# Macaron block with routed experts: router transposes two units later, dense outputs spread, first scatter in three steps, second roots on VectorE

## The reference, cut to what matters

```
x = x + 0.5 * ffn(layernorm(x))
x = x +       attention(layernorm(x))
x = x + 0.5 * ffn(layernorm(x))

ffn:  logits = x @ router_w.T ; e = argmax(logits)          # one of 8 experts per row
      out = square(relu(x @ fc[e])) @ proj[e]               # 128 -> 512 -> 128
attention: q, k = split(x @ Wqk + bqk); v = k; 16 heads of 8 channels
      causal windows of max(4, 128 / 2**h) keys for head h
      out = softmax(q k' / sqrt(8), masked) v
      gates = softmax(x @ Wgate + bgate)  (one per head)
      result = (out * gates) @ Wproj + bproj
```

## Time and profile before

| | |
|---|---|
| median of three runs | 444.68 us (442.11 to 444.8) |
| profiled execution | 440.26 us, of which the span is 438.5 us |
| mean granted TensorE clock in it | 0.952 |
| PE busy | 357.5 us, 82% of the span |
| DVE busy | 281.5 us, 64% |
| ACT busy | 263.5 us, 60% |
| POOL busy | 256.1 us, 58% |

### The profile page before, as it was taken

One profiled execution on the slowest core, in us unless ns is written; L12 is line 12 of the kernel. 1 busy time (PEld: TensorE's weight loads), 2 busy tenths in 40 slices (PEclk: granted clock), 3 DMA queues, 4 the chain that ended last, 5 costly groups with the idle time before them and its releaser, 6 DMA issues.

```text
span 438.5 us, 9118 instructions
## 1 busy us (share of the span) xinstructions
PE 357.5 (82%) x2634; PEld 333.2 (76%) x2643; DVE 281.5 (64%) x617; ACT 263.5 (60%) x684; POOL 256.1 (58%) x289
## 2 busy tenths in 40 slices
PE   5951049999998798779999999999475699999990
PEld 5941049999998477568879797989474699999990
DVE  4696014545566486999777979899996555545540
ACT  3370077667676586445787878686363367677650
POOL 5227747000174778487483847574977977765451
PEclk9999999999999999996999999999696599999996
DMA  9993113222242287417081822224022545722210
GB/s 244 405 270 91 54 54 102 77 66 61 78 120 73 67 184 153 100 33 161 19 169 29 172 61 40 58 41 98 12 100 96 140 125 160 198 82 63 58 29 1
DMA packets 82492, 45.40 MB, mean 104 GB/s; under 512 B 47117, under 2 KB 77455, under 8 KB 82209
## 3 DMA queue, kind: packets, MB, share of 16 engines
q1 hardware_dynamic: 77312, 34.38, 31.3%
q0 software_dynamic: 4864, 10.51, 7.6%
q10 hardware_dynamic: 288, 0.19, 0.2%
HBM read 24.48 MB, written 21.01 MB: 104 GB/s over the span
## 4 chain that ended last, share of the span: by engine, by line
PE 53%; POOL 20%; issue 9%; DVE 6%; ACT 5%; DMA 4%; SPq 1%; POOLq 0%; ACTq 0%; DVEq 0%
PE bank L1355 14%; PE bank L1346 14%; POOL rows_d L527 7%; PE bank L1433 5%; POOL late_rows_d L527 4%; POOL late L546 4%; PE bank L1465 3%; PE bank L1317 3%; PE bank L1443 2%; PE bank L1337 2%; PE bank L1306 2%; ACT sq L643 2%; ACT rows L626 2%; POOL rstd L574 2%; DMA rows<-in_x 1%
## 5 line engine op out<-in xcount | busy, mean ns | idle before, releaser
L1013 DVE TENSOR_SCALAR hT<-bank 128x512 f32<-128x512 f32 x80 | 55.3, 691 | 69.2 <-PE bank L1346 69.0
L1346 PE MATMUL bank<-xT,fcb 128*128 128x128 f32 x640 | 88.3, 283 | 5.6 <-ACT xT L659 5.6
L1355 PE MATMUL bank<-wo,hT 128*128 x640 | 87.9, 281 | 2.3 <-ACT hT L675 2.3
L1346 PEld LDWEIGHTS bank<-xT,fcb 128*128 128x128 f32 x640 | 81.2, 199 | 6.4 <-ACT xT L659 6.4
L1355 PEld LDWEIGHTS bank<-wo,hT 128*128 128x128 f32 x640 | 78.5, 193 | 3.1 <-issue 3.1
L669 ACT ACTIVATE fcb<-fc 128x512 f32 x80 | 50.2, 629 | 45.9 <-PE bank L1346 45.5
L546 POOL DMA_INDIRECT late<-y_d,slot x32 | 31.1, 973 | 51.1 <-DMA y_d<-ys 41.8
L537 POOL DMA_INDIRECT out_rows<-late x40 | 39.3, 983 | 24.9 <-DVE late L1022 17.9
L675 ACT ACTIVATE hT<-hT 128x512 f32<-128x512 f32 x80 | 50.1, 627 | 5.6 <-DVE hT L1013 5.2
L1433 PE MATMUL bank<-kT,qT 128*128 128x128 f32 (+4 forms) x256 | 48.5, 318 | 2.3 <-ACT late L754 2.0
L754 ACT ACTIVATE late<-bank,nmax 128x128 f32<-128x128 f32 (+2 forms) x128 | 46.5, 408 | 5.7 <-DVE nmax L1075 4.3
(11 more groups left out here) (158 smaller groups left out, 712.2 us busy)
## 6 DMA issues: line engine op xcount, KB each, us to landing
ks<-k_d SPq DMA_DIRECT2D x32, 192.0 KB, 3.3
late_rows_d<-hT SPq DMA_DIRECT2D x5, 1028.0 KB, 7.7
rows_d<-late SPq DMA_DIRECT2D x2, 1280.0 KB
xs<-rows_d SPq DMA_DIRECT2D x20, 128.0 KB
y_d<-ys SPq DMA_DIRECT2D x40, 64.0 KB
xs<-late_rows_d SPq DMA_DIRECT2D x20, 128.0 KB
fc<-in_w_fc SPq DMA_DIRECT2D x1, 2048.0 KB, 15.7
k_d<-qkg SPq DMA_DIRECT2D x8, 192.0 KB, 2.2
```

Of the source, the lines that this page charges most:

```text
L1013: nc.vector.tensor_scalar(hT[:, v, :, :].rearrange("p k c -> p (k c)"), bank[v][:, :], 0.0, None, ALU.max).then_inc(r_s, 1)
L1346: mm = pe.matmul(bank[v][:, k * 128:(k + 1) * 128], fcb[:, v, k * 128:(k + 1) * 128], xT[:, v, :], start=True, stop=True)
L1355: mm = pe.matmul(bank[OUT_BANK[f] + v][:, 0:128], hT[:, v, k, :], wo[:, ds(e, 1), k, :], start=(k == 0), stop=(k == KT - 1))
```

## The change

Four parts.

- The first segment's scatter is issued in three steps of six tiles, each with its own wait for the normalising, which now signals after each six tiles; the semaphore's later counts are raised to match.
- The second segment's roots are computed by DVE with `spread`, behind `place_blocks(0, 1)`, instead of by POOL. POOL has one root less there. ACT does the second segment's normalising behind the mask casts instead of ahead of them.
- The router's transposes, copies and logits are placed at slots 3, 4 and 4, 5 instead of 1, 2 and 2, 3, except in batch 6.
- `outputs(i, 0)` and `outputs(i, 1)`, which stood one behind the other in slot 3 ahead of `turn_probs`, are placed in slot 2 and in slot 3, behind `turn_probs` and the projections.

```diff
 # POOL
-            for h in range(2):
-                roots(h + 1, SEG[0][h])
-                if h == 0:
-                    pool.wait_ge(zero_s, 48)
-                scatter(0, h, SEG[0][h], h + 1)
+            roots(1, SEG[0][0])
+            pool.wait_ge(zero_s, 48)
+            for k in range(3):
+                scatter(0, 0, slice(6 * k, 6 * k + 6), k + 1)
+            scatter(0, 1, SEG[0][1], 4)
             gather(0, 0, 14)
-            roots(3, LN2[0])
+            roots(2, LN2[0])
...
 # ACT
-            def normalise_rows(h, t0, t1):
-
-                act.wait_ge(root_s, h + 1)
+            def normalise_rows(r, t0, t1):
+
+                act.wait_ge(*r)
                 for t in range(t0, t1):
                     ins = act.activation(xn[:, t, :], xn[:, t, :], ACT.Copy, scale=rstd[:, t:t + 1])
-                if t1 == SEG[0][h].stop:
-                    ins.then_inc(norm_s, 1)
+                ins.then_inc(norm_s, 1)
...
-                if i >= 2 and n in (1, 2):
-                    route_copy(1, 2 * (i - 2) + n - 1, (2, 2))
+                at = 1 if i == 6 else 3
+                if i >= 2 and n in (at, at + 1):
+                    route_copy(1, 2 * (i - 2) + n - at, (2, 2))
...
                 if g >= 13:
-                    normalise_rows(0, 6 * (g - 13), 6 * (g - 12))
+                    normalise_rows((root_s, 1), 6 * (g - 13), 6 * (g - 12))
...
-            normalise_rows(1, SEG[0][1].start, N_TILES)
-
             act.wait_ge(late_const_s, 16)
             act.activation(identb[:, :], ident, ACT.Copy).then_inc(masks_s, 1)
             a, b_ = CONST_AT["mask_first"][0], CONST_AT["mask_rest"][1]
             act.activation(maskb[:, :], cst[:, a:b_], ACT.Copy).then_inc(masks_s, 1)
+            normalise_rows((rstd_s, 1), SEG[0][1].start, N_TILES)
...
 # DVE
-            scaled_variance(3, SEG[0][1])
             choose(0, 1, 3)
             count_blocks(0, 1, 3)
             bases(0, 1)
             place_tokens(0, 1, 3)
             place_blocks(0, 1)
+            spread(3, SEG[0][1])
...
 # PE, slot (i, n)
                 if n == 0 and i:
                     outputs(i - 1, 3)
-                if n == 3:
-                    outputs(i, 0)
-                    outputs(i, 1)
                 if n == 5:
                     outputs(i, 2)
                 turn_probs(i, n)
...
+                if n in (2, 3):
+                    outputs(i, n - 2)
                 if i >= 2:
-                    g = 2 * (i - 2)
-                    if n in (2, 3):
-                        route_logits(1, g + n - 2, 2)
-                    if n in (1, 2):
-                        route_turn(1, g + n - 1, (2, 2))
+                    g, at = 2 * (i - 2), 1 if i == 6 else 3
+                    if n in (at + 1, at + 2):
+                        route_logits(1, g + n - at - 1, 2)
+                    if n in (at, at + 1):
+                        route_turn(1, g + n - at, (2, 2))
```

More of the change, by code:

```diff
@@ L342, in normalise_batch @@
         def normalise_batch(eng, i):
-            eng.wait_ge(root_s, len(SEG[0]) + 1 + [4 * i < tiles.stop for tiles in LN2].index(True))
+            eng.wait_ge(root_s, len(SEG[0]) + [4 * i < tiles.stop for tiles in LN2].index(True))
             if i:
@@ L579, in window @@
                 if i in (0, 2):
-                    roots(4 + i // 2, LN2[1 + i // 2])
+                    roots(3 + i // 2, LN2[1 + i // 2])
                 if i + 2 < B:
@@ L586, in window @@
                 if 3 <= i:
-                    roots(3 + i, batch(i - 3))
-                    normalise(pool, 1, (root_s, 3 + i), batch(i - 3))
+                    roots(2 + i, batch(i - 3))
+                    normalise(pool, 1, (root_s, 2 + i), batch(i - 3))
                 add_output_bias(i)
@@ L606, in _ @@
             pool.wait_ge(no_token_s, 16 * -(-NB // FILL))
-            scatter(1, 0, slice(0, 16), 6)
-            scatter(1, 0, batch(4), 7)
+            scatter(1, 0, slice(0, 16), 8)
+            scatter(1, 0, batch(4), 9)
             for i in range(5, B):
-                roots(i + 6, batch(i))
-                normalise(pool, 1, (root_s, i + 6), batch(i))
-            scatter(1, 1, SEG[1][1], 10)
+                roots(i + 5, batch(i))
+                normalise(pool, 1, (root_s, i + 5), batch(i))
+            scatter(1, 1, SEG[1][1], 12)
             put_out(range(NB))
```

## The result

The changed kernel took 449.06 us (median of 5 runs, 445.58 to 450.16) and the kernel before 444.68 (5 runs, 442.11 to 446.08): a ratio of 1.0088, 95% interval 1.0045 to 1.0131. The forecast was 440.5. Medians are of all runs, while a ratio leaves out the executions in a slower state that every kernel shows now and then. The profiled execution took 445.58 for a span of 443.8; 5.3 more than the 438.5 of before. Both profiles are of the fastest run of their kernel: the profile of before has a mean granted TensorE clock of 0.952, while 28 runs of it on the last chip have 0.921 to 0.944.

A forecast was written before the change was run, and what follows sets the result against it. PE was taken to bound the attention loop, with POOL ending stretches at the start. Start -7.7 plus attention +3.6 gave -4.1 us: 440.5 from the median 444.68, range 435 to 446.

The forecast's parts named there:

- -4.1: Whole kernel: -7.7 us for the start plus 3.6 for the attention loop, so a faster kernel.
- The start: First feed-forward stage and all behind it: three scatter steps and DVE's second roots give -7.7 us, between -7.3 and -8.4.
- DVE's roots: Start: second roots on DVE end at 43.8, delay no slot, and let POOL go on at 49.5 instead of 58.78.
- from scatter to scatter it is 1.27: Start, POOL: spacing (50.66 - 28.99) / 17, so 18 scatters from 26.6 end at 49.2.
- The 68.2: Start: time by which the last scatter, issued at 66.0, lands.
- Three steps: Start: the first scatter needs only six normalised rows, so it starts at 26.6, 2.4 us earlier.
- The wait for the gate: Attention loop: PE reaches outputs 0 at T + 10.8 and stalls 1.0 to 1.9 us; laps 21.45, +1.1 in batches 3 to 6.
- batch 2: Attention loop: its T, the start of unit 5's transposes, comes at 218.3 instead of 219.07, a gain of 0.75 us.
- The forecast's rule: Attention loop: lap is the gate's end after T, plus 0.14 lag, plus 8.92 of PE work behind it.
- 3.6: Attention loop: net loss in us, from +1.1 in each of batches 3 to 6 and -0.75 in batch 2.
- rival B: Attention loop: clock falls at each new stall, 1.7 us in each of five batches, 8.5 in all; total 449.1; chance 0.08.
- The 0.46 disappears inside the new stall: Attention loop: PE's idle 0.46 us ahead of the router's logits, waiting for ACT's copy, vanishes in the gate stall.

The follow-up runs named there:

- `steps_only`: Kernel before with only the first scatter in three steps, second roots still on POOL: ratio 0.9917 to the kernel before.
- `roots_only`: Kernel before with only the second roots on DVE and the casts moved, first scatter in one step: ratio 0.9979 to the kernel before.
- `start_third`: Changed kernel with the attention loop of before, so only the start parts, on the last chip: 437.58 us, ratio 0.9825 to the kernel before.
- `filler_again`: Changed kernel plus six unused 96-column products ahead of the gate wait in batches 2 to 5, last chip: 444.63 us, ratio 0.9998 to before.
- `change_again`: The changed kernel itself, unaltered, run again on the last chip: 448.06 us, ratio 1.0092 to the kernel before.
- `outputs_back`: Changed kernel with outputs 0 and 1 back together in unit 3, router pieces still late: ratio 1.0083 to the kernel before.
- `start_only`: Changed kernel with the attention loop of before, so only the start parts, in the first group: ratio 1.002 to the kernel before.
- `start_again`: Start parts alone once more, attention loop of before, in the second group: ratio 0.9981 to the kernel before.
- `outputs_moved`: Changed kernel with the router pieces back at their old units, so only the outputs are new in attention: ratio 1.0194 to the kernel before.

## Why the prediction was wrong

Its sign was wrong: -4.1 was forecast, about +4 came (449.06 - 444.68 = +4.4; 448.06 - 444.38 = +3.7). The start was priced 1.6 too high, and, the larger fault, the sum has no term for the clock.

**The start: mechanism right, size 1.6 too large.** The first scatter (26.54 to 27.17 in the kernels with steps, forecast 26.6), DVE's roots (44.19, forecast 43.8), the second series without a gap and the first product bound by its load were as forecast. The step that was off is "from scatter to scatter it is 1.27". It was read from a series that hardly meets DVE's centring of the later rows; started 1.8 earlier, the second and third scatter meet it, and (49.88 - 27.17) / 17 is 1.34, or 1.1 more over the 17. The 68.2 at which the last scatter was to land follows from no row, and nothing is added up from it. Three steps gave 1.2 instead of 2.4 (`steps_only`), DVE's roots 4.9 (`roots_only`). The roots behind the stage start at 134.17 instead of 140.23: -6.1, not -7.7. In full runs the whole start is worth -6.8 (`start_third`).

**The wait for the gate: right.** T + 11.67 to 12.72 against a mean of 12.39, laps at a full clock of 20.98 and 21.31 against 21.45, batch 2 from the start's -6.06 to -6.70, so -0.64 against -0.75. The forecast's rule, lap = gate + 0.14 + 8.92, holds with the clock held by the filler too: there the gate ends at T + 12.15, 13.18 and 12.62, and the laps are 21.12, 22.14 and 21.59 (by the rule 21.21, 22.24 and 21.68). The gate itself was later in `filler_again` than the forecast took it, in batch 4 by 0.6.

**The failed step: the clock, put at nothing in the sum.** "-7.7 + 3.6 = -4.1" prices the new stalls at their own length only. What they do to the granted clock stands in rival B alone, at 0.08, with the reason "the stalls are single and short". The runs showed that single stalls of 1.43 to 2.02 are followed by a half-rate stretch in six of seven laps of the two profiles of the changed kernel (only the stall of 1.56 was not), and that this is worth at least 3.4 us (`filler_again`). Rival B had the mechanism; that its 449.1 is also the time measured is in part luck, since it took -7.7 for the start and five falls of 1.7, and its profile shows -6.1 and two falls, of 1.7 and 4.8. The row that was used against it, PE idle for 0.92 of 2 us at a clock of 1.00, is one wait of 1.07 for ACT (216.92), and the row for it is a wait of 1.86 with the clock at 0.58 behind it. A forecast stall of 1.0 to 1.9 lay between the two, in five rounds, so these rows did not rule the rival out, and 0.08 was too little for it. Its price, 1.7 a fall, was about the least: PE's busy time in a lap grew by 1.7 where the clock was 0.93, by 3.3 (23.00 - 19.69) at 0.86 and by 4.8 at 0.81. The Trainium skill, TensorE: Matmul & The Clock Gate, section HAM oscillation, says of a kernel that waits for a DMA in every round of its loop that the clock drops in every round; the trace agrees, with four laps of four in `change_again`. The waits of that case are longer than the 1 to 2 us here, which the prediction's "by it this rival would be the outcome" left out.

**An omission: ACT behind the router.** "The 0.46 disappears inside the new stall" treated the router's wait as pure loss. `outputs_back` shows that it hid a wait of 1.09 for the exponentials. In the four laps of the changed kernel no such wait for ACT is left beside the gate's, so it cost nothing there. It is why the laps of `outputs_back`, with the router moved and the outputs not, are longer than the old ones.

**The sum, made anew** on the last chip: -6.8 for the start, +10.5 for the attention loop. Of the 10.5, 3.4 go away with the filler of four batches, so the clock costs at least that; the rest is 7.1. The four laps of `filler_again` are 87.79 - 81.33 = 6.5 longer than those of `start_third`: by 0.8, 1.8 and 1.3 with the filler, at full clock, and by 2.6 in the one without, whose clock fell (some 1.7 of it, as in the other laps at 0.93). So an estimate for the clock is 3.4 + 1.7 = 5.1, and for the order itself 5.4, where the forecast had 3.6. The spans of the two profiles differ by 4.2 only (441.3 and 437.1), because the part behind the key store is 2.2 longer in `start_third`; whether it is in the other runs too is not shown. How often the clock falls differs from profile to profile, and what decides it between waits of equal length is open; so is why the part behind the key store of batch 7 differs between profiles (139.7 in that of before, 141.1 in that of `filler_again`, 143.3 = 437.1 - 293.80 in that of `start_third`).

## What to carry to other kernels

When a move turns PE's scattered idle time into one wait per round, price the wait twice: its own length, and the half-rate stretch that may follow it, which cost PE's busy time 1.7 to 4.8 more here. If such a wait can't be avoided, dummy products ahead of it are worth a trial: six of 96 columns kept the clock at 1.00 here in six laps of six. An existing small wait may be the cover of a larger one: before moving it, ask what PE will reach earlier and which engine is still using that. A scatter's spacing holds only beside the same neighbours: before moving a series of them, look at which DVE operations it will meet; and parts of a change should be timed apart, since here one part was worth 6.8 us and the other lost 10.5.

## What the runs showed that was not expected

- The clock fell behind short waits of an engine that was otherwise busy: 2.02 and 1.76 in the changed kernel, 1.03 in `filler_again`, and on the first two chips behind 0.46 (`start_only`) and 0.47 (`start_again`) alone; in other laps waits of the same size left it at 1.00 (1.56 in the changed kernel, 1.94 in `outputs_moved`, 0.46 in 21 of the 24 laps of the old order).
- Six products of 96 columns ahead of a wait of 1 to 2 us, which compute nothing, made the kernel 3.4 us faster.
- The same indirect scatter takes POOL 0.96, also with the DMA engines full (share 1.01), and 1.15 or 1.81 where it starts inside a DVE operation on two tensors of 1.07 or 1.09: it then ends 0.83 to 0.85 behind the end of that operation, in eleven profiles of eleven.
